# One program that works batch by batch through first stage, attention and router, in place of three programs one after the other

## The reference

```python
# first layer: rows and context rounded to fp8 in blocks, then multiplied
xq = quant_dequant_act_1x128(layernorm(x))        # scale per row and 128 columns
wq = quant_dequant_weight_128x128(ctx)            # scale per 128x128 block
x  = x + einsum('emk,enk->emn', xq, wq)
# second layer
hidden = layernorm(x)
h = rmsnorm(hidden, attn_norm_w)
q, k, v = h @ q_w.T, h @ k_w.T, h @ v_w.T         # 16 query heads, 4 key heads, 128 wide
q, k = rope(rmsnorm(q)), rope(rmsnorm(k))
attn = softmax(causal(q @ k.T / sqrt(128))) @ v
hidden = hidden + attn @ o_w.T
tok = rmsnorm(hidden, ffn_norm_w)
probs = softmax(tok @ gate_w.T); top 2 of 8 experts, weights normed
out = x + hidden + sum over experts of weight * (silu(tok @ wg.T) * (tok @ wu.T)) @ wd.T
```

## Time and profile before

| | us |
|---|---|
| profiled execution, its time | 1700.5 |
| its span, first to last instruction | 1698.5 |
| start to the first score | 355.8 |
| attention, from there to the last output added | 873 |
| router, to the start of dispatch | 81 |
| dispatch and experts | 387.5 |
| of it dispatch, to the first gather of rows | 48 |
| experts, one tile of 128 rows | 8.07 |

### The profile page before, as it was taken

How to read it: one execution, slowest core, us unless ns; L and a number is a source line. 1 busy time by engine, 2 the same in 40 slices (tenths; PEclk the granted TensorE clock), 3 DMA queues, 4 the chain that set the end, 5 groups by cost and what they waited for, 6 DMA issues and landing times. The chain is left out here.

```text
span 1698.5 us, 23301 instructions
## 1 busy us (share of the span) xinstructions
PE 1287.3 (76%) x6606; PEld 981.5 (58%) x6606; DVE 952.0 (56%) x2751; ACT 604.7 (36%) x1969; POOL 501.9 (30%) x635
## 2 busy tenths in 40 slices
PE   0221113478998999989999899999845389999996
PEld 0010101367887878878888788887645056566653
DVE  8979798256775667757767677767422611111110
ACT  1111201245555555555555455555231012222221
POOL 2423150234334333333342433322110023333332
PEclk9995555699999999999999999999955589999998
DMA  6010102312111121111120211100099023333332
GB/s 241 0 75 0 75 0 88 147 51 75 51 51 44 45 76 51 51 38 51 53 74 1 81 51 51 39 14 1 2 371 281 1 50 68 68 63 63 69 67 38
DMA packets 31525, 115.25 MB, mean 68 GB/s; under 512 B 3296, under 2 KB 4064, under 8 KB 27296
## 3 DMA queue, kind: packets, MB, share of 16 engines
q0 software_dynamic: 10848, 24.65, 8.1%
q10 hardware_dynamic: 3744, 51.45, 7.8%
q1 hardware_dynamic: 16800, 37.58, 6.3%
HBM read 82.21 MB, written 31.46 MB: 67 GB/s over the span
## 5 line engine op out<-in xcount | busy, mean ns | idle before, releaser
L623 PE MATMUL bank<-w_hi,hTb 128*128 128x512 f32 (+1 forms) x1024 | 284.9, 352 | 22.6 <-DMA hTb<-hT_scratch 18.4
L775 ACT ACTIVATE prob<-bank,bias,scale 128x128 f32<-128x128 f32 (+3 forms) x256 | 157.2, 616 | 215.8 <-DVE prob L894 215.8
L623 PEld LDWEIGHTS bank<-w_hi,hTb 128*128 128x128 f32 x1024 | 184.1, 193 | 46.4 <-DMA hTb<-hT_scratch 18.8
L576 POOL TENSOR_TENSOR prob<-prob,rtotal 128x128 f32<-128x128 f32 (+2 forms) x192 | 116.6, 616 | 269.4 <-DVE rtotal L900 265.4
L1322 PE MATMUL gu<-we,xT 128*128 x624 | 193.5, 464 | 1.0 <-ACT xT L1366 0.8
L910 DVE TENSOR_TENSOR pT_lo<-bank,pT_hi 128x512 fp32r<-128x512 f32 (+3 forms) x256 | 119.5, 489 | 131.1 <-ACT pT_hi L783 123.0
L623 PE MATMUL bank<-w_lo,hTb 128*128 128x512 f32 (+1 forms) x512 | 174.6, 341 | 0.0
L550 POOL TENSOR_TENSOR r<-r,rot 128x640 f32<-128x640 f32 x64 | 100.0, 1562 | 224.2 <-DVE v_lo L871 224.2
L1322 PEld LDWEIGHTS gu<-we,xT 128*128 128x128 f32 x624 | 116.7, 192 | 60.4 <-issue 3.3
L783 ACT ACTIVATE pT_hi<-bank 128x512 fp32r<-128x512 f32 (+3 forms) x256 | 104.7, 437 | 119.1 <-PE bank L659 119.0
L894 DVE TENSOR_SCALAR_CACHE_REDUCE prob<-bank,nscale 128x128 f32<-128x128 f32 (+3 forms) x256 | 134.8, 545 | 18.2 <-PE bank L650 18.1
(11 more groups left out here) (222 smaller groups left out, 2755.8 us busy)
## 6 DMA issues: line engine op xcount, KB each, us to landing
hTb<-hT_scratch ACTq DMA_DIRECT2D x16, 2048.0 KB, 8.2
we<-in_wexp ACTq DMA_DIRECT2D x8, 2176.0 KB, 34.4
stage<-in_wqkvo SPq DMA_DIRECT2D x40, 256.0 KB, 3.0
xs<-in_x SPq DMA_DIRECT2D x4, 1024.0 KB, 14.4
cs<-in_ctxT SPq DMA_DIRECT2D x4, 1024.0 KB, 11.3
out<-xs SPq DMA_DIRECT2D x4, 1024.0 KB, 4.5
hT_scratch<-hT_hi SPq DMA_DIRECT2D x4, 1024.0 KB, 3.9
hT_scratch<-hT_lo SPq DMA_DIRECT2D x4, 1024.0 KB, 6.3
```

What stands on the lines that cost most here:

```text
L576: nc.gpsimd.tensor_tensor(p, p, rtotal[:, 4 * h + q:4 * h + q + 1].broadcast_to([P, KEYS[q]]), ALU.mult).then_inc(prob_ready, 1)
L623: last = nc.tensor.matmul(o, hT[:, a, k, t * P:(t + 1) * P], wkv(c, k) if kv else wq(c, k), start=(k == 0 and n == 0), stop=(k == KC - 1 a ...
L775: nc.scalar.activation(prob[h % 2][:, P_AT[q]:P_AT[q] + KEYS[q]], bank[SC + q % 2][:, 0:KEYS[q]], ACT.Exp, bias=bias[:, 4 * h + q:4 * h + ...
```

## The change

The three programs `quant_projection`, `attention` and `router` become one, `mixer`, written out without loops. Its 16 iterations now have the batch outside and the group of heads inside. Only batch 0 has its first stage ahead of the iterations. The first stage of batch b+1 is cut in small units that stand in the iterations of batch b (table `FRONT`), and the router of batch b-1 in the last iteration of batch b (`ROUTE`). For the last batch the router stands behind the iterations.

```diff
+FILL = {(0, 1): [("u", 4)], (0, 2): [("q", 0)], (0, 3): [("kv", 0), ("q", 1)],
...
+        (2, 1): [("q", 3)], (2, 2): [("kv", 3), ("o", 0)], (2, 3): [("n", 0), ("o", 1)],
+        (3, 1): [("m", 0), ("o", 2)], (3, 2): [("o", 3)], (3, 3): [("t", 0), ("t", 1), ("t", 2), ("t", 3)]}
+FRONT = ({(0, 1): [("cm", 0)], (0, 2): [("cs", 0)], (0, 3): [("cv", 0)],
+          (1, 1): [("cr", 0), ("cv", 1)], (1, 2): [("cd", 0), ("cr", 1), ("cv", 2)], (1, 3): [("cd", 1), ("cr", 2), ("cv", 3)],
...
+         {(0, 1): [("xa", 0)], (0, 2): [("xv", 0), ("xa", 1)], (0, 3): [("xr", 0), ("xv", 1)],
+          (1, 1): [("xd", 0), ("xr", 1)], (1, 2): [("xt", 0), ("xd", 1), ("xh", 2)], (1, 3): [("xp", 0), ("xa", 2)],
...
```

The products of the first stage are plain fp32 on numbers that ACT has scaled back, four matmuls into one bank, and DVE adds the sum once. The rounding is on DVE alone, four steps for each 128x512 block:

```diff
+                last = nc.tensor.matmul(product_bank(n)[:, :], xT[:, k, :], cb[:, k, :], start=(k == 0), stop=(k == KC - 1))
...
+            def round_fp8(z):
+                own.chain(nc.vector.tensor_scalar(xm[:, :].bitcast(U32), z.bitcast(U32), EXPONENT_BITS, None, ALU.bitwise_and))
+                own.chain(nc.vector.tensor_scalar(xm[:, :], xm[:, :], FP8_LEAST_NORMAL, None, ALU.max))
+                own.chain(nc.vector.scalar_tensor_tensor(z, xm[:, :], FP8_ROUND, z, ALU.mult, ALU.add))
+                return nc.vector.scalar_tensor_tensor(z, xm[:, :], FP8_ROUND, z, ALU.mult, ALU.subtract)
```

```diff
-                for n, (a, c) in enumerate(SPLITS):
-                    last = nc.tensor.matmul(bank[PV][:, j * P:S], v[b % 2][a][:, j, :], pT[c][:, PT_AT[j]:PT_AT[j] + QS[j]],
-                                            start=(j == 0 and n == 0), stop=(j == TT - 1 and n == 2))
+                nc.tensor.matmul(bank[PV][:, j * P:S], v[it % 2][:, j, :], pT[:, PT_AT[j]:PT_AT[j] + QS[j]],
+                                 start=(j == 0), stop=(j == TT - 1)).then_inc(pv_step, 1)
```

The split rows stay in SBUF for the four iterations of a batch. The weights are split during batch 0 (DVE now makes the low part, L960, where POOL did) and saved; the other three batches load the split weights back, 5 MB for each iteration, by SP:

```diff
+                if HKV <= it + 2 < NIT:
+                    load_q(it + 2)
+                    load_kv(it + 2)
+                if it >= HKV:
+                    load_o(it)
```

```diff
-            pe.wait_ge(w_in, 16 * E)
...
+                pe.wait_ge(w_ready, pe.value_load(eneed[0:1, i:i + 1], min_val=1, max_val=E))
```

More of the change, by code:

```diff
@@ L31 @@
 CH = 512
-RING = 5
 FP8_MAX = 448.0
@@ L82, in build @@
         h2_dram = nc.dram_tensor("h2_scratch", (B * S, D), F32, kind="Internal").ap()
[L83 to L100, removed]
@@ new lines, with need, units @@
+RING_A = 6
+def need(engine, sem, count):
+    if count > 0:
+        engine.wait_ge(sem, count)
+def units(it, h, place):
+    b, g = divmod(it, HKV)
+    slot = (h, place)
+    if b + 1 < B:
+        yield from FRONT_FIRST[g].get(slot, ())
+    if g == HKV - 1 and b:
+        yield from ROUTE_FIRST.get(slot, ())
+    for kind, i in FILL.get(slot, ()):
+        if (kind != "o" or it) and (it + 1 < NIT or kind in "ou"):
+            yield kind, i
+    if b + 1 < B:
+        yield from FRONT[g].get(slot, ())
+    if g == HKV - 1 and b:
+        yield from ROUTE.get(slot, ())
+    if it + 2 < HKV:
+        yield from SPLIT_Q.get(slot, ())
+    if 1 <= it <= HKV:
+        yield from SPLIT_O.get(slot, ())
@@ L517, in fill, with pieces @@
-        def fill(h, place, handlers, first, last):
-            for kind, i in FILL.get((h, place), ()):
-                if kind in handlers and not (first and kind == "o") and not (last and kind not in "ou"):
-                    handlers[kind](i)
+            return w[i][:, QKV + h, :]
+        def pieces(c):
+            if c < KC:
+                return ((slice(0, CH), wcol[:, c:c + 1]),)
+            return tuple((slice(i * 2 * HD, (i + 1) * 2 * HD), wcol[:, 2 * (c - KC) + i:2 * (c - KC) + i + 1]) for i in range(2))
@@ L583, in attend @@
                     normalise(it, h, 1)
-                    fill(h, 1, work, first, last)
+                    for kind, i in units(it, h, 1):
+                        if kind in work:
+                            work[kind](i)
                     normalise(it, h, 2)
-                    fill(h, 2, work, first, last)
-                    fill(h, 3, work, first, last)
-                if b == 0:
-                    for c in range(QKV, NCH):
-                        split_lo(NCH * g + c, c)
-                if b == 2 and not (isinstance(g, int) and g == HKV - 1):
-                    for c in range(QKV):
-                        split_lo(NCH * (g + 1) + c, c)
@@ L595, in _ @@
-            pool.sem_inc(rope_added, FREE[rope_added])
-            for c in range(QKV):
-                split_lo(c, c)
-            nc.gpsimd.memset(n15[:, :], 1.5).then_inc(pool_own, 1)
-            for t in range(TT):
-                add_rope(0, t)
-            newton(0)
-            batches(pool, attend)
+                    for place in (2, 3):
+                        for kind, i in units(it, h, place):
+                            if kind in work:
+                                work[kind](i)
@@ L676, in output @@
[L676 to L687 removed]
+                    need(pe, at_lo, s)
@@ L1285, in experts, with _ @@
         block = ctx.enter_context(nc.Block())
+        @block.sync
+        def _(sp):
+            for e in range(E):
+                sp.wait_ge(w_in[e], 16)
+                sp.sem_inc(w_ready, 1)
         @block.gpsimd
```

1391 lines of the change are left out of this document (736 added, 655 removed), and 11 rows, old and new, of tables (FILL, FRONT, ROUTE).

## The result

| | us | against before |
|---|---|---|
| before | 1701.97 median of 4 (1699.84 to 1703.56) | |
| after | 1628.66 median of 4 (1623.92 to 1629.54) | ratio 0.9564, 95% interval 0.9543 to 0.9586 |
| forecast | 1520, range 1455 to 1605 | |

The change makes the kernel 4.4% faster. I had forecast 10.6%, and the measured time lies 24 us above my range.

What follows compares the result with a forecast made beforehand. DVE was taken to bound the first stage and PE the attention. Front 130, attention 973, router's rest 22, dispatch and experts 393.5 made 1518.5 us; with 2.0 us beside the span, 1520, range 1455 to 1605.

Steps and rivals of the forecast that it cites:

- Front: Batch 0's first stage ahead of the attention: 130 us in place of 355, bounds 118 and 150.
- router's rest: Router of batch 3, left behind the last output: 22 us in place of 81, bounds 18 to 30.
- dispatch and experts: Program's end, with expert weights now loading from dispatch on: 393.5 us against 387.5 before, bounds 387 to 405.
- Loads of split weights at nothing: Attention: 2 MB loads at 8.2 us, issued more than a head's turn ahead of use, cost nothing.
- Values +16: Attention: plain fp32 value products add 0.25 us for each of 64 heads, +16 us, bounds 0 and +30.
- −5 for the wait that is gone: Attention: PE no longer waits for the low parts of the probabilities, 5 us less.
- First-stage products +41: Attention: first-stage products of three batches, 48 at 0.86 us each, add 41 us of PE time.
- "New waits", +20: Attention: 5 us for each of three crowded iterations and 5 us for late weight blocks in batch 0; bounds 0, +100.
- second rival: Attention: 24 rounding blocks hold up the row maxima, 55 us, or 101 with slow steps beside POOL; 1585 us, 23%.
- my term for PE's work: Attention: PE time added for values +16, first-stage products +41, transpositions +10 and router of three batches +16.
- Better cover: Attention: more independent work between scores and exponentials removes PE's 43 us of idling; 1462 us, 13%.
- Slower: PE's clock falls in the attention, deciding from 181 us of PE work at the lower level; time passes 1701, 3%.

Runs made afterwards that it cites:

- run 3: Changed kernel with the weight splitting of groups 1 to 3 on 8 columns in place of 512, loads and stores kept: 1610.6 us, ratio 0.9467.
- run 5: Changed kernel with the old unit order, 7 buffers, rounding of batches 1 to 3 and splitting of groups 1 to 3 on 8 columns: 1535.5 us, ratio 0.9009.
- run 1: Changed kernel with the kernel before's order of units between the scores, and 7 buffers in place of 6 for attention results: 1568.4 us, ratio 0.9228.
- run 4: Kernel before with only the products of probabilities and values made plain fp32: 1719.8 us, ratio 1.0115.
- run 8: Changed kernel in the old order with 7 buffers, one of four first-stage products per tile in batches 1 to 3: 1544.4 us, ratio 0.9067.
- run 2: Changed kernel in its own order, the 24 rounding blocks of batches 1 to 3 on 8 columns in place of 512: 1604.8 us, ratio 0.9443.
- run 9: Changed kernel with 7 buffers and only the first of the four outputs moved back one place: 1587.0 us, ratio 0.9319.
- run 10: Changed kernel in the old order but 6 buffers, last output one step earlier, plain fp32 values: 1600.4 us, ratio 0.9403.
- run 11: Changed kernel in the old order but 6 buffers, last output one step earlier, values as three split products: 1608.2 us, ratio 0.9445.
- run 6: Changed kernel with 7 buffers and only the last of the four outputs back between the third and fourth q transpositions: 1629.4 us, ratio 0.9575.

## Why the prediction was wrong

*Front, router's rest, dispatch and experts*: right in their sums, as the first table shows, and the front in its steps too: the first product at 50.1 us for 48, the last over at 70.2 for 70, the split rows ready at 88.3 for 90, the first score at 122.9 for 124. One small wait of the first iteration had no term: 5 to 7 us for the low part of k, in every run, without the splitting too (runs 3 and 5).

*Loads of split weights at nothing*: right, 5.1 to 7.4 us for the megabyte transfers, and PE waits once, 3.3 us in run 1, in the last iteration.

*Values +16, and −5 for the wait that is gone*: together +11; alone, in run 4, they cost 20.5. The +16 is about right (1.1 us an iteration), the −5 was no gain, and the 4 us above the 16 are no more than run 4 spent longer at the lower clock level (7). The mechanism was right, the credit for the wait was not.

*First-stage products +41*: run 8 prices 36 of the 48 at 24 to 27 us, so all at 32 to 36. A little too dear, though the matmuls themselves cost what the rows say.

*"New waits", +20, the step that failed.* The term held the new work's waits and put the order of the old units at nothing. The part I had thought of, roundings and weight blocks, costs 33 us in run 5. Of it the roundings alone, 21 to 24 us in run 2, are my second rival's mechanism, at under half of its lower price of 55. A block has a median of 0.42 + 0.43 + 0.69 + 0.69 = 2.2 us in after's trace. Its second step took 1.66 to 1.68 us in 9 of the 24 blocks, each time beside one and the same addition on POOL, and 0.43 in the 15 where POOL did nothing:

```profile
151.44 0.42 DVE L888 TENSOR_SCALAR xm<-cb 128x512 uint32<-128x512 uint32 x1
151.60 1.67 POOL L385 TENSOR_TENSOR r<-r,rot 128x640 f32<-128x640 f32 x1 [0.48 <-DVE rot L1007]
151.89 1.67 DVE L889 TENSOR_SCALAR xm<-xm 128x512 f32<-128x512 f32 x1
...
158.16 0.43 DVE L889 TENSOR_SCALAR xm<-xm 128x512 f32<-128x512 f32 x1
```

The other part I had not seen at all: **the order in `FILL`, 60 us (run 1)**, of which 42 are the first output's one place (run 9). I took the table as a list of what is new, where it also moved what was there. The rule that would have caught it follows from my own account of the kernel: all engines run in order and meet at semaphores, so a unit's bank must be free and its operand ready when PE comes to it. The diff showed the line, and batch 0's outputs needed weights whose splitting stands in the place just before.

In medians: 1520 was forecast and 1628.7 came, 109 us more. The order has 60 of them. Roundings and splitting have about 13 over my 20, values about 9. Some 26 stay, or over 30 if the first-stage products are taken at what they cost. The clock has 12 of them: its sum over 40 slices (as under run 1) is 26.0 us in run 5 and 14.0 in the kernel before, and my term for PE's work had held no time at the lower level beyond that of before. Run 5's first iteration also has 17.7 us of idle PE in it, where that of before had 6.5. No run takes these two apart, and they may be one thing; 7 of run 4's 20.5 for the values may be clock as well. The rest stays open.

*The rivals.* "Better cover" never showed: the waits for exponentials doubled. "Slower" was far off, but its mechanism was at work in small: of the 124 us by which PE's busy time grew, 33 are the lower level (47.4 against 14.0), which leaves 91 of work for my 83. The signs that I had named for the second rival both came, long rounding steps and over 60 us of PE waits, and the order still cost more. The sign that pointed at the order was batch 3's iteration, 58.2 us for 54 to 56. The Trainium skill (FP8 and Floating Point Precision, TensorE Precision Notes) counts four passes for true fp32, where the split form is three products; I worked out +43 us from it and set that aside for +16. Run 4 with 20.5 us bears out the price by the rows here, not the one by the count of passes. The other rule that I had weighed (SBUF — State Buffer, Who interferes with whom), on the ports that DVE and GpSimd share, agrees with those nine long steps, and would by itself not have given the time.

## What to carry to other kernels

When a change rewrites a table of order, compare the places of the old units first, and for each one that moved ask what bank, buffer or operand it needs and who frees it; here one output moved by one place was worth 42 us over 15 iterations, more than all the rounding that was moved in. A buffer count can be such a table's hidden reason: the early outputs save a seventh buffer of 4 KB for each partition, and in the old order that buffer was worth 30 to 32 us. And an iteration without the new work (batch 3 here) is the place to look first: what is longer there is not the new work's fault.

## What I had not expected

- The plain fp32 values are the slower form where PE is the bound (+20.5 us in the kernel before), and the faster one where DVE is crowded (8 us in run 10 against run 11): the 120 us of DVE work that they save are worth more there than what they cost PE.
- Waits can cost twice: of the 62.9 us by which the old order shortens the attention, 22.6 are the same matmuls running at a higher share of the 2.4 GHz level. The two don't move in step: run 9 took away 33 us of idle PE and 7 us of busy time, run 6 had more idle time and a higher clock.
- Of the four outputs, moving the last alone gives 0 and moving the first alone 42 (runs 6 and 9); moving all four gives 60.
- The version of run 1 beats both kernels: 1568.4 us, 7.7% under the kernel before.
